# One core, a non-local block over 32 images: the first key projection takes its 256 moving columns as two runs of 128

## The reference

```python
q = einsum('bchw,dc->bdhw', x, theta_w) + theta_b          # 256 x 1024 per image
xpool = maxpool2(x)                                        # 1024 channels x 256
k = einsum('bchw,dc->bdhw', xpool, phi_w) + phi_b          # 256 x 256 per image
v = einsum('bchw,dc->bdhw', xpool, g_w) + g_b
p = softmax(einsum('bdn,bdm->bnm', q, k) * 256 ** -0.5, axis=-1)
vp = einsum('bdm,bnm->bdn', v, p)
out = einsum('bdhw,cd->bchw', vp, z_w) + z_b + x
```

## Time and profile before

| what | value |
|---|---|
| median of the runs | 2045.76 us |
| lowest and highest run | 2045.47 and 2046.67 us |
| span of the profiled execution, first to last instruction | 2040.4 us |
| TensorE matmuls, busy | 2026.8 us, 99% of the span |
| VectorE, ScalarE, GpSimd, busy | 1558.1, 1300.0, 1366.5 us |
| granted TensorE clock, mean | 1.000 |

### The profile page before, as it was taken

The page is one execution under the profiler, slowest core; times in us unless marked ns, Lnnn a source line. Parts: engine busy times, 40 slices in busy tenths (PEclk is TensorE's granted clock), DMA queues, the critical chain, the costliest instruction groups (busy, mean ns, idle before and its releaser), DMA issues.

```text
span 2040.4 us, 48999 instructions
## 1 busy us (share of the span) xinstructions
PE 2026.8 (99%) x17790; PEld 2024.5 (99%) x17790; DVE 1558.1 (76%) x2625; ACT 1300.0 (64%) x2228; POOL 1366.5 (67%) x828
## 2 busy tenths in 40 slices
PE   9999999999999999999999999999999999999998
PEld 9999999999999999999999999999999999999998
DVE  8878777787777877777877778777787777787777
ACT  6666666666566665666666666666666566666663
POOL 4577666776666766667766677666677666776663
PEclk9999999999999999999999999999999999999999
DMA  7565656746556565566565664656656556656554
GB/s 243 191 212 184 213 169 214 236 170 210 175 207 232 180 210 185 186 226 210 181 212 171 215 237 169 209 177 207 232 180 210 184 187 226 209 182 214 170 193 166
DMA packets 213963, 407.27 MB, mean 200 GB/s; under 512 B 12720, under 2 KB 17840, under 8 KB 213936
## 3 DMA queue, kind: packets, MB, share of 16 engines
q1 hardware_dynamic: 213792, 406.90, 59.0%
q10 hardware_dynamic: 144, 0.01, 0.0%
HBM read 272.64 MB, written 134.22 MB: 199 GB/s over the span
## 4 chain that ended last, share of the span: by engine, by line
PE 97%; DVE 2%; POOL 0%; DMA 0%; issue 0%; ACT 0%; SPq 0%; DVEq 0%; POOLq 0%
PE bank L967 97%; DVE x_top L755 0%; DVE pt_raw L736 0%; DMA x<-x 0%; DVE x_bot L755 0%; DVE pooled L708 0%; POOL att_lo L631 0%; POOL x_split_lo L613 0%; POOL att_f L626 0%; DVE x L755 0%; PE bank L974 0%; SPq L265 0%; DVE q_lo L714 0%; ACT att_hi L425 0%; DVE xp_lo L851 0%
## 5 line engine op out<-in xcount | busy, mean ns | idle before, releaser
L613 POOL TENSOR_TENSOR x_split_lo<-x,x_split_hi 128x1024 fp32r<-128x1024 f32 x255 | 614.6, 2417 | 248.4 <-ACT x_split_hi L386 226.7
L967 PE MATMUL bank<-x_split_hi,theta_hi 128*128 128x256 f32 x2048 | 565.8, 276 | 3.1 <-POOL x_split_lo L613 2.0
L967 PE MATMUL bank<-x_split_lo,theta_hi 128*128 128x256 f32 x2048 | 565.7, 276 | 0.0
L967 PE MATMUL bank<-x_split_hi,theta_lo 128*128 128x256 f32 x2048 | 565.7, 276 | 0.0
L967 PE MATMUL bank<-att_hi,z_hi 128*128 128x256 f32 x1792 | 495.4, 276 | 3.6 <-DVE x_bot L755 2.5
L967 PE MATMUL bank<-att_hi,z_lo 128*128 128x256 f32 x1792 | 494.9, 276 | 0.0
L967 PE MATMUL bank<-att_lo,z_hi 128*128 128x256 f32 x1792 | 494.9, 276 | 0.0
L736 DVE STREAM_TRANSPOSE pt_raw<-probs 32x256 f32<-32x256 f32 x1024 | 445.9, 435 | 18.4 <-ACT probs L489 1.8
L631 POOL TENSOR_TENSOR att_lo<-att_f,att_hi 128x768 fp32r<-128x768 f32 x191 | 282.6, 1487 | 159.4 <-ACT att_hi L425 159.4
L967 PEld LDWEIGHTS bank<-x_split_hi,theta_hi 128*128 128x128 f32 x2048 | 384.6, 188 | 3.5 <-issue 3.5
L967 PEld LDWEIGHTS bank<-x_split_hi,theta_lo 128*128 128x128 f32 x2048 | 384.6, 188 | 0.0
(11 more groups left out here) (76 smaller groups left out, 4390.0 us busy)
## 6 DMA issues: line engine op xcount, KB each, us to landing
x<-x SPq DMA_DIRECT2D x258, 512.0 KB, 3.9
x_top<-x SPq DMA_DIRECT2D x128, 512.0 KB, 7.0
out<-x_top SPq DMA_DIRECT2D x128, 512.0 KB, 3.3
x_bot<-x SPq DMA_DIRECT2D x126, 512.0 KB, 5.2
out<-x_bot SPq DMA_DIRECT2D x126, 512.0 KB, 6.6
x_top<-theta_wt SPq DMA_DIRECT2D x4, 256.0 KB, 5.4
x_top<-g_wt SPq DMA_DIRECT2D x4, 256.0 KB, 5.4
x_bot<-z_wt SPq DMA_DIRECT2D x4, 256.0 KB, 6.2
```

The source lines that it names most:

```text
L613: nc.gpsimd.tensor_tensor(flat(lo), flat(x_chunk(s, c)), raw(flat(hi)), ALU.subtract).then_inc(x_ready, 1)
L967: last = nc.tensor.matmul(dst, stationary(a), moving(b), start=start and n == 0, stop=stop and n == len(PRODUCTS) - 1, skip_group_check=re ...
```

## The change

The call of `project_k()` in the prologue becomes a call of a new function, `project_first_k()`. For each of the two blocks of planes it walks the eight channel blocks twice, once for the pooled columns 0 to 127 and once for 128 to 255. Each product is made of the same three matmuls, with 128 moving columns in place of 256, so it issues 96 matmuls with 96 weight loads where 48 with 48 stood. The same elements are added in the same order. Only the first product of the first half opens the accumulation, and `k_done` is raised after the last matmul as before.

```diff
+            def project_first_k():
+                for m in range(DT):
+                    for w in range(2):
+                        at = slice(w * MH, (w + 1) * MH)
+                        for kt in range(KT):
+                            last = product(k_bank[:, m * M + w * MH:m * M + (w + 1) * MH],
+                                           lambda a: phi[a][:, kt, m * P:(m + 1) * P], lambda b: xp[b][:, kt, at],
+                                           kt == 0 and w == 0, kt == KT - 1, w > 0)
+                last.then_inc(k_done, 1)
...
             keep_busy(o_x[1], 24)
             pe.wait_ge(w_ready, (PHI + 1) * PIECES)
             pe.wait_ge(xp_ready, 2)
-            project_k()
+            project_first_k()
             project_q(0, 1, 2)
```

## The result

The changed kernel takes 2049.18 us (median of 10 runs), the kernel before 2044.78 us in the 10 runs made beside it: ratio 1.0026, 95% interval 1.0018 to 1.0035, so 3.7 to 7.2 us slower, 5.3 in the middle; the two medians lie 4.4 us apart. Forecast were +5.5 us, and slower. Single executions of the kernel before differ among themselves by as much as the change costs (2041.67 to 2046.67 us).

The account below looks back on a forecast made before the run. TensorE was taken to bound the kernel, with matmul records over 99% of the span. Replacing 5.44 us of projection by 10.89, passed on whole, was taken as +5.5: 2045.76 + 5.5 = 2051.3 us, range 2050.0 to 2052.2, with rivals 2049.9 to 2062.2.

Parts of the forecast that it names:

- The price: First key projection: each 128-column fp32r matmul with its load costs 113.4 ns, 10.89 us for 96, +5.4 us.
- the excess of 6.7 ns: Key projection's 256-column matmuls: 113.4 ns against 106.7 for the columns alone, the difference put down to the weight load.
- Passing on: From the first key projection to the kernel's end: TensorE's delay reaches the end 1 to 1.
- a sign of being wrong: VectorE's stretch to 88 us starting later but ending less late would show the prediction wrong.
- The pace behind: TensorE behind the first key projection: matmuls at 117.5 ns against 113.4; a quicker pace might give back up to 0.9 us.
- the 0.9 us: Some 220 matmuls up to 60.9 us: possible gain from a quicker pace, not counted on, put into the lower end.
- The 115.5 ns: Stretch behind the first key projection: 129 matmuls recorded in 14.9 us, read as 115.5 ns each.
- The columns rule: Rival at the first key projection: load hides behind columns or costs the zeros' pair, 2045.8 to 2048.1 us; chance 0.13.
- The dear short matmul: Rival at the first key projection: short fp32r matmuls cost more than their load, +10.6 to +16.3 us, about 2060.8; chance 0.30.
- the rival of the series: Rival set for the follow-up series: short fp32r matmuls pass columns at half rate, 0.83 ns each; no chance given.

Follow-up runs that it names:

- uneven halves: Kernel before with the first key projection in two runs of 192 and 64 columns instead of one of 256: 2049.42 us, ratio 1.0029.
- series with fewer columns of weights: Kernel before plus unused fp32r matmul series with 128, 64 or 32 weight columns; 128 moving columns took 110 ns at 128 weights, 62.5 at 64; no kernel time given.
- plain delay: Kernel before with 65 more matmuls on zeros ahead of the unchanged first key projection: 2049.30 us, ratio 1.0028.
- 32 projections: Kernel before with all 32 key projections, not only the first, split into two runs of 128 columns: 2205.34 us, ratio 1.0803.
- the series: Kernel before plus unused series of 48 fp32r matmuls with 64 to 512 moving columns and of bf16 matmuls on zeros, in the prologue: 2114.5 us.
- the quarters: Kernel before with the first key projection in four runs of 64 columns, 192 matmuls with 192 loads: 2077.47 us, ratio 1.0168.

## Why the prediction was right

**The price.** That "the load costs 90 to 113 ns and can't hide behind 53 ns of columns" was the step that decided, and it held: 112.0 ns measured, 113.4 taken, 10.75 us for 96 against the 10.89 worked out, so +5.2 us against +5.4. It was argued from two rows, the load records of bf16 and fp32r (98 and 188 ns) and the order of load and matmul after an idle stretch. The uneven halves and the series with fewer columns of weights show what these could only suggest, that the price doesn't follow the moving columns and falls with the load. The rule of the Trainium skill (TensorE: Matmul & The Clock Gate, section LDWEIGHTS), columns of weights over 1.2, gives 107 ns and 53 for 64; at full clock the runs agree within 3 ns for 128 (110) and within 7 to 9 for 64 (60 to 62.5). At the clock's lower level a pair took 213 ns, which is not the same 107, so here the rule holds for full clock alone. The 81 ns per pair that the same page of the Trainium skill gives in its section Back-to-back issue gap is not what fp32r does here (112.0 ns with 128 columns).

**A sign read wrongly.** The prediction took the excess of 6.7 ns over the columns at 256 as coming from the load. The runs are against it: with 512 columns, where a load of 110 ns is far from the limit, the excess grew to 19 ns (232.5 - 213.3). The conclusion that the load sets the pace didn't rest on it, but the choice of 113.4 ns within 90 to 113 did, and the sentence "the load is the only other thing in the stream" was wrong. That the forecast came as near as 0.3 us of the projection's +5.2 was therefore in part luck; any value of the bounds above 100 ns would have given the same answer, slower. What slows long fp32r streams stays open.

**Passing on.** One to one, as costed: +5.2 us in the projection, 5.3 us in the ratio; the plain delay of 5.37 us gave 5.7 (3.3 to 8.2), and 32 projections gave 162 us. The prediction named a sign of being wrong, that VectorE's stretch to 88 us starts later but ends less late. The chain of the profile after looks like it, 6.43 us later at att_f and 4.8 at its next long piece, but the two pieces begin at different matmuls; the same matmul is 7.40 us later there, and 5.02 in the uneven halves without a fall of the clock.

**The pace behind.** It stayed at the slower one, 2.88 us for the 24 query matmuls; the 0.9 us were rightly not counted on. The 115.5 ns read from the window of 14.9 us were a misreading: its 129 matmuls include those that reach over its edges, and their starts, from 45.79 to 60.87 us, lie 117.8 ns apart.

**The rivals.** The columns rule would have needed pairs below 100 ns and is out. The dear short matmul is out for 128 columns, as four passes would have cost 213 ns and 112.0 were measured; columns at half the rate, the rival of the series, would have given 53 ns at 64 columns, where the uneven halves have 109. Yet a larger cost than the one given to it exists one step on. With 64 columns the clock fell, which no rival had, and the kernel lost 34 us.

## What to carry to other kernels

Before splitting a matmul's moving columns, compare them with its weight load: in fp32r a load of 128 columns of weights took about 110 ns here at full clock, as long as 256 moving columns, so 64 to 224 moving columns cost the same and a split in two doubled the time. In a kernel whose chain is TensorE alone, price the change where it is made and pass it on whole. Look at the granted clock of the stretch too before a cost is scaled: by its loads alone the split in four would have cost three times what the split in two did (16.1 us of projection against 5.2), and with the fall of the clock it cost six times (31.0 us).

## What the runs showed that I had not expected

- In two kernels a stretch of fp32r matmuls with 64 columns lost the clock though TensorE was never idle: in the quarters it was 1.00 from 29.6 to 33.0 us and 0.53 from 36.7 to 74.2. With 128 columns (10.7 us in the prologue, and in all images) it stayed at 1.00, and so it did with 192 and 64 columns in turn. What the fall depends on wasn't tested.
- The load follows TensorE's clock: 112 ns a pair with 64 columns at 2.4 GHz, 213 at 1.2.
- One fp32r matmul of 512 columns costs 232.5 ns in this kernel, more than two of 256 with their loads (226.7).
- Two executions out of twelve of one kernel took 9.4 and 9.9 ms, where the same kernel took 2048.6 us on another chip. In the one that has a trace the matmuls go by at 656 ns in the mean from 26 to 500 us and at about 410 ns after 6000 us, at a clock recorded as 1.00. The cause wasn't looked for.
